# Group statistics of a GroupNorm by a lane shuffle and copies on VectorE in place of products, in a two-layer attention kernel

## The chip, the cores and the metric

One core of one Trainium2 chip runs the whole program. The metric is the device time of one execution in microseconds (us); lower is better. Engines are named as in the profile: PE is TensorE's matmul (PEld its weight load), DVE is VectorE, ACT is ScalarE, POOL is GpSimd, SP is SyncE, which here only issues DMAs. Every engine runs its own list of instructions strictly in order and waits for the others on semaphores.

## The reference

Two self-attention blocks one after the other, on x of shape (4, 64, 32, 32), float32. Each block is

```python
h = group_norm(x, 32 groups)          # 2 channels x 1024 pixels in a group; eps 1e-5, then 1e-6
q, k, v = conv1x1(h)                  # 64 -> 64 channels each, with biases
s = softmax(q^T k / sqrt(64))         # 1024 x 1024 for each image
x = x + conv1x1(s v) + bias
```

So there are eight units of work: four images in each of two layers. An image of the second layer needs the finished image of the first.

## The kernel before

**Layout.** An image lies on 128 partitions: partitions 0 to 63 hold the 64 channels of the first 512 pixels, partitions 64 to 127 the same channels of the other 512. A group of two channels therefore lies on four partitions: c, c^1, and the same two 64 further on. 

**Stages of a unit u.**
1. Statistics: DVE takes each partition's mean and variance (`gn_own`, L440 to L444). PE multiplies the means by a constant matrix that averages over a group (`group_mean_of`, L604 to L606); DVE forms the deviation of each partition from it (`gn_about`, L446 to L454); PE averages again (`group_var_of`, L608 to L610); DVE adds epsilon (`gn_var`, L456 to L459); POOL takes the power -0.5 (`root`, L234 to L236); DVE makes the gain and the shift (`gn_affine`, L461 to L470); ACT applies them and writes h (`apply_norm`, L312).
2. PE projects q and k into ps_scores[0] (`project`, L612) and v times the output weights into ps_misc (`project_v`, L622). ACT copies the high parts, DVE the low parts (L472, L479). SP swaps the halves of the keys by DMA.
3. Row maxima: for each of 8 tiles of 128 queries PE forms rough scores into ps_max (`max_scores`, L628) and DVE takes their maximum (`row_max`, L486). There is one ps_max, so PE's tile m waits until DVE has finished tile m-1 (`next_max`, L756). PE turns the maxima (`turn_max`), ACT stages them (`stage_max`), and SP writes them as rows into q_row with two DMAs, one for each half (`place_rows`, L189).
4. Scores: for each of 8 tiles of keys PE forms the exact scores (`scores`, L644) and ACT the exponentials (`exp`, L345). POOL adds the eight tiles up one by one (`add`, L238, seven additions a unit). PE multiplies by the values into ps_attn (`values`, L668).
5. Closing: when POOL's seventh addition is done PE forms the sums of the softmax (`denominators`, L681), ACT copies them, DVE takes reciprocals in four chunks (`reciprocal`, L501), and POOL multiplies and adds the residual (`finish`, L249), which it does between its third and fourth addition of the next unit.

**Order.** All orders are written out by hand. In iteration w of the main loop PE does the scores and values of unit w, the row maxima of unit w+1, the statistics' products and the projections of unit w+2, and the sums of unit w-1. The statistics' products exist in w = 0 to 5 ("prep"): one pair stands between scores tile 0 and tile 1 (L771), the other after tile 1 (L774). DVE's order in an iteration (L541 to L577) is: row_max 2, gn_about, row_max 3, gn_var and gn_affine, row_max 4, reciprocal, row_max 5, reciprocal, the low parts, two reciprocals, row_max 6 and 7, row_max 0 and 1 of the unit after, gn_own of unit w+3. POOL's order (L289 to L295) is: `root(w + 2)`, additions 1 to 3, finish of unit w-1, additions 4 to 7. Since it is in order, the root of iteration w stands behind the seventh addition of iteration w-1.

**Start.** PE runs `keep_warm` products that nobody reads (20, then 16, L711 and L716), around the first products of the statistics and of the weights (`setup`), before it projects unit 0.

The tail (units 6 and 7 and the closing of unit 7) has no statistics in it.

Of the kernel before, what the change touches and what calls it, by code (L numbers as in the profile page):

```python
# [5 lines left out]
ALU = mybir.AluOpType  # L6
# [24 lines left out]
def attention_pair(nc, x, layer_params, consts, out):  # L31
# [16 lines left out]
    GN = 7  # L48

    with ExitStack() as ctx:  # L50
# [15 lines left out]
        const_sb = sb("const_sb", [P, 2 * P])  # L66
        ident, half_group_mean = const_sb[:, 0:P], const_sb[:, P:2 * P]
# [4 lines left out]
        stats6 = sb("stats6", [P, 6])  # L72
        own = sb("own", [P, 2])
        neg_mean = sb("neg_mean", [P, 1])
        dev = sb("dev", [P, 1])
        var_about = sb("var_about", [P, 1])
# [37 lines left out]
        mean_mm = sem("mean_mm")  # L114
        var_mm = sem("var_mm")
# [51 lines left out]
        def last_row(unit):  # L167
            return 32 * (unit // 2 + 1)
# [4 lines left out]
        def _(sp):  # L173
# [15 lines left out]
            def place_rows(u):  # L189
                sp.wait_ge(max_staged, u + 1)  # L190
                if u < 2:
                    sp.wait_ge(rows_zero, u + 1)
                for n in range(2):
                    row = q_row[u % 2][n * C:n * C + 1, :].bitcast(F32).rearrange("p (t n) -> p t n", t=JS)
                    sp.dma_start(row, max_rows[n * JS:(n + 1) * JS, :].bitcast(F32)).then_inc(row_in[u % 2], 16)
# [104 lines left out]
        def _(act):  # L300
            act.dma_start(const_sb[:, :], consts).then_inc(consts_in, 16)
# [137 lines left out]
        def _(dve):  # L439
            def gn_own(u):  # L440
                base = GN * u
                dve.bn_stats(stats6[:, :], xs[:, slot(u)]).then_inc(gn_step, 1)
                dve.wait_ge(gn_step, base + 1)
                dve.bn_aggr(own[:, :], stats6[:, :]).then_inc(gn_step, 1)  # L444

            def gn_about(u):  # L446
                base = GN * u
                dve.wait_ge(mean_mm, u + 1)
                dve.tensor_scalar(neg_mean[:, :], ps_misc[:, 0:1], -2.0, None, ALU.mult).then_inc(gn_step, 1)
                dve.tensor_scalar(dev[:, :], ps_misc[:, 0:1], -2.0, own[:, 0:1],  # L450
                                  ALU.mult, ALU.add).then_inc(gn_step, 1)
                dve.wait_ge(gn_step, base + 4)
                dve.tensor_scalar(var_about[:, :], dev[:, :], dev[:, :], own[:, 1:2],
                                  ALU.mult, ALU.add).then_inc(gn_step, 1)  # L454

            def gn_var(u):  # L456
                dve.wait_ge(var_mm, u + 1)
                dve.tensor_scalar(var_eps[:, :], ps_misc[:, 1:2], 2.0, EPS[u // B],  # L458
                                  ALU.mult, ALU.add).then_inc(var_ready, 1)  # L459
# [59 lines left out]
            gn_own(0)  # L519
            gn_about(0)  # L520
            gn_var(0)
# [3 lines left out]
            gn_own(1)  # L525
            gn_about(1)
# [4 lines left out]
            gn_var(1)  # L531
# [5 lines left out]
            gn_own(2)  # L537
# [3 lines left out]
            for w in range(UNITS):  # L541
# [5 lines left out]
                if prep:  # L547
                    gn_about(w + 2)
                if nxt:
                    row_max(w + 1, 3)  # L550
                if prep:
                    gn_var(w + 2)
                    gn_affine(w + 2)
# [20 lines left out]
                if w + 3 < UNITS:  # L574
                    if w + 3 >= B:
                        dve.wait_ge(final_done, w + 3 - B + 1)
                    gn_own(w + 3)  # L577
# [21 lines left out]
        def _(pe):  # L599
# [3 lines left out]

            def group_mean_of(u):  # L604
                pe.wait_ge(gn_step, GN * u + 2)
                pe.matmul(ps_misc[:, 0:1], half_group_mean, own[:, 0:1], start=True, stop=True).then_inc(mean_mm, 1)  # L606

            def group_var_of(u):  # L608
                pe.wait_ge(gn_step, GN * u + 5)
                pe.matmul(ps_misc[:, 1:2], half_group_mean, var_about[:, :], start=True, stop=True).then_inc(var_mm, 1)  # L610
# [29 lines left out]
            def turn_max(u):  # L640
                pe.wait_ge(max_ready, u + 1)
                pe.transpose(ps_misc[0:TILES, 0:P], neg_max[u % 2][:, :], ident).then_inc(max_turned, 1)
# [69 lines left out]
            pe.wait_ge(consts_in, 16)  # L712
# [167 lines left out]
```

## Time and profile before

| | |
|---|---|
| median of 3 runs | 206.66 us (206.65, 206.66, 210.21) |
| profiled execution | 207.81 us |
| its span from the first to the last instruction | 206.0 us |
| PE busy | 93% of the span |
| DVE, ACT, POOL busy | 66%, 51%, 76% |
| granted TensorE clock, mean | 0.997 |

The profile is of one execution, a little longer than the median. Times inside it are microseconds from the start of its span; the 1.8 us between its time and its span lie outside what the profile shows.

### The profile page before, as it was taken

How to read it: one execution, taken by the hardware profiler on the slowest of the kernel's cores; microseconds unless marked ns; L12 is line 12 of the kernel's file. 1: busy time of each engine (PE TensorE's matmuls, PEld its weight loads, DVE VectorE, ACT ScalarE, POOL GpSimd, SP SyncE). 2: the span in 40 equal slices, each digit the busy share in tenths (PEclk: the TensorE clock that was granted, in tenths of full speed). 3: DMA queues.
4: the chain of work that ended last, by engine and by line, in shares of the span. 5: the costliest groups of instructions: out<-in, count | busy, mean ns of one | idle time of the engine just before them, and what ended most of it. 6: DMA issues, size and time to landing. Idle time of an engine off the chain costs nothing.

```text
span 206.0 us, 3281 instructions
## 1 busy us (share of the span) xinstructions
PE 192.3 (93%) x1248; PEld 104.0 (50%) x1248; DVE 136.1 (66%) x186; ACT 105.1 (51%) x147; POOL 156.0 (76%) x93
## 2 busy tenths in 40 slices
PE   8989887999999999999999999999999997999950
PEld 8956654645455544554644555554555443444410
DVE  1369957556796749775886679567965485007974
ACT  2458435564655557535854375646555363628310
POOL 1244207799599997998799989997999869998913
PEclk9999999999999999999999999999999999999998
DMA  6224020400021000400040004000211000100011
GB/s 198 108 51 97 8 55 0 102 1 5 2 61 44 1 0 11 93 4 0 0 102 4 0 0 103 3 0 2 63 42 52 5 0 0 52 0 3 0 51 51
DMA packets 4719, 7.06 MB, mean 34 GB/s; under 512 B 800, under 2 KB 1760, under 8 KB 4704
## 3 DMA queue, kind: packets, MB, share of 16 engines
q1 hardware_dynamic: 4272, 6.33, 12.2%
q10 hardware_dynamic: 432, 0.53, 0.9%
q8 instruction: 10, 0.16, 0.3%
q14 instruction: 5, 0.04, 0.1%
HBM read 1.58 MB, written 1.05 MB: 13 GB/s over the span
## 4 chain that ended last, share of the span: by engine, by line
PE 77%; DVE 8%; POOL 8%; issue 3%; ACT 2%; POOLq 0%; DVEq 0%; ACTq 0%
PE ps_attn L677 23%; PE ps_max L637 9%; PE ps_scores L657 6%; POOL prob_sum L247 6%; PE ps_scores L661 5%; PE ps_scores L659 5%; PE ps_scores L665 5%; PE ps_scores L617 4%; PE ps_scores L602 4%; PE ps_misc L625 4%; DVE neg_part L490 3%; PE ps_misc L684 3%; DVE prob_sum L516 2%; ACT probs L350 1%; DVE rden L586 1%
## 5 line engine op out<-in xcount | busy, mean ns | idle before, releaser
L247 POOL TENSOR_TENSOR prob_sum<-prob_sum,probs 128x1024 f32<-128x1024 f32 x44 | 104.5, 2375 | 13.3 <-ACT probs L350 9.0
L490 DVE TENSOR_REDUCE neg_part<-ps_max 128x2 f32<-128x1024 f32 x59 | 71.8, 1218 | 34.7 <-PE ps_max L638 34.7
L350 ACT ACTIVATE probs<-ps_scores 128x1024 f32<-128x1024 f32 x64 | 63.0, 1024 | 48.4 <-PE ps_scores L666 45.1
L677 PE MATMUL ps_attn<-probs,vals 128*64 128x512 f32 x256 | 61.9, 604 | 0.0
L506 DVE RECIPROCAL rden<-den 128x128 f32<-128x128 f32 x28 | 25.1, 926 | 14.9 <-ACT den L356 14.9
L637 PE MATMUL ps_max<-keys,q_hi 64*128 64x512 f32 x59 | 27.7, 470 | 3.6 <-DVE neg_part L490 3.0
L677 PEld LDWEIGHTS ps_attn<-probs,vals 128*64 128x64 f32 x256 | 15.8, 136 | 27.3 <-issue 19.9
L638 PE MATMUL ps_max<-keys,q_hi 64*128 64x512 f32 x59 | 27.7, 469 | 0.0
L657 PE MATMUL ps_scores<-q_hi,keys 64*128 64x512 f32 x64 | 26.3, 411 | 0.0
L658 PE MATMUL ps_scores<-q_hi,keys 64*128 64x512 f32 x64 | 26.3, 411 | 0.0
L665 PE MATMUL ps_scores<-q_row,ones_r 64*128 64x512 f32 x64 | 25.0, 391 | 0.0
L666 PE MATMUL ps_scores<-q_row,ones_r 64*128 64x512 f32 x64 | 25.0, 391 | 0.0
L660 PE MATMUL ps_scores<-q_lo,keys 64*128 64x512 f32 x64 | 25.0, 391 | 0.0
L659 PE MATMUL ps_scores<-q_lo,keys 64*128 64x512 f32 x64 | 25.0, 391 | 0.0
L661 PE MATMUL ps_scores<-q_hi,keys 64*128 64x512 f32 x64 | 25.0, 390 | 0.0
L662 PE MATMUL ps_scores<-q_hi,keys 64*128 64x512 f32 x64 | 24.9, 389 | 0.0
L637 PEld LDWEIGHTS ps_max<-keys,q_hi 64*128 64x128 f32 x59 | 10.8, 183 | 24.4 <-DVE neg_part L490 12.4
L236 POOL TENSOR_TENSOR rstd<-var_eps,minus_half 128x1 f32<-128x1 f32 x8 | 4.4, 552 | 23.7 <-DVE var_eps L458 23.7
L247 POOL TENSOR_TENSOR prob_sum<-probs 128x1024 f32<-128x1024 f32 x8 | 19.1, 2388 | 0.0
L657 PEld LDWEIGHTS ps_scores<-q_hi,keys 64*128 64x128 f32 x64 | 11.8, 185 | 4.6 <-ACT probs L350 2.4
L661 PEld LDWEIGHTS ps_scores<-q_hi,keys 64*128 64x128 f32 x64 | 11.8, 184 | 2.5
L665 PEld LDWEIGHTS ps_scores<-q_row,ones_r 64*128 64x128 f32 x64 | 11.8, 184 | 2.5
(88 smaller groups left out, 308.5 us busy)
## 6 DMA issues: line engine op xcount, KB each, us to landing
keys<-keys SPq DMA_DIRECT2D x32, 128.0 KB, 2.3
xs<-x_dram SPq DMA_DIRECT2D x4, 256.0 KB, 4.3
out_dram<-xs SPq DMA_DIRECT2D x3, 256.0 KB, 2.1
layer<-layers_dram ACTq DMA_DIRECT2D x2, 194.5 KB, 4.7
q_row<-max_rows SPq DMA_DIRECT2D x16, 2.0 KB
out_dram<-xs SPq DMA_DIRECT2D x4, 64.0 KB, 1.6
const_sb<-consts_dram ACTq DMA_DIRECT2D x1, 128.0 KB, 3.6
```

Source lines behind the costliest of these rows:

```text
L247: pool.tensor_tensor(prob_sum[u % 2][:, :], first[:, :], probs[t][:, :], ALU.add).then_inc(added, 1)
L350: act.activation(probs[t][:, :], ps_scores[t % 2][:, :], ACT.Exp, scale=SCALE).then_inc(exp_done, 1)
L490: dve.tensor_reduce(neg_part[u % 2][:, at:at + JS + 1:JS], ps[:, :].rearrange("p (h n) -> p h n", h=2), AX.X, ALU.max, negate=True).then_i ...
L506: dve.reciprocal(rden[:, chunk(c)], den[:, chunk(c)]).then_inc(rden_done, 1)
L637: pe.matmul(ps[:, 0:HALF], q[0:C, mine], k[0:C, cols], start=True, stop=True)
L638: pe.matmul(ps[:, HALF:N], q[C:P, mine], k[C:P, cols], start=True, stop=True).then_inc(max_mm, 1)
L657: pe.matmul(left, k[top, a:a + P], q[top, 0:HALF], start=True, stop=False)
L658: pe.matmul(right, k[low, b:b + P], q[low, 0:HALF], start=True, stop=False)
L659: pe.matmul(left, k[top, a:a + P], ql[top, :], start=False, stop=False)
L661: pe.matmul(left, k[top, a + HALF:a + HALF + P], q[top, 0:HALF], start=False, stop=False)
L665: pe.matmul(left, ones_r[top, :], row[top, :], start=False, stop=True)
L677: mm = pe.matmul(ps_attn[half * C:(half + 1) * C, :], v, probs[t][:, cols], start=(t == 0), stop=(t == TILES - 1))
```

## The change

The products of the statistics go, with their semaphores and the averaging matrix. DVE does it all in one function: it takes the six numbers that `bn_stats` leaves on each partition, swaps neighbouring lanes with one shuffle, copies both sets to the other half of the partitions with two copies, and aggregates the four sets in one `bn_aggr`. Epsilon and the negated mean are taken in the same place. The function stands where `gn_own` stood, so it handles unit w+3 at the end of iteration w. `gn_affine` moves up from behind row_max 3 to behind row_max 2. The DMA of the constants brings the identity alone. The two row DMAs become one. At the start PE has 6 idle products in place of 16. POOL's and ACT's orders are not touched.

```diff
+    PAIRED = [lane ^ 1 for lane in range(32)]
...
-        const_sb = sb("const_sb", [P, 2 * P])
+        ident = sb("ident", [P, P])
...
-            return 32 * (unit // 2 + 1)
+            return 16 * (unit // 2 + 1)
...
-                for n in range(2):
-                    row = q_row[u % 2][n * C:n * C + 1, :].bitcast(F32).rearrange("p (t n) -> p t n", t=JS)
-                    sp.dma_start(row, max_rows[n * JS:(n + 1) * JS, :].bitcast(F32)).then_inc(row_in[u % 2], 16)
+                rows = q_row[u % 2][0:P:C, :].bitcast(F32).rearrange("p (t n) -> p t n", t=JS)
+                sp.dma_start(rows, max_rows[:, :].bitcast(F32)).then_inc(row_in[u % 2], 16)
...
-            act.dma_start(const_sb[:, :], consts).then_inc(consts_in, 16)
+            act.dma_start(ident[:, :], consts[:, 0:P]).then_inc(consts_in, 16)
...
-            def gn_own(u):
+            def gn_group(u):
                 base = GN * u
-                dve.bn_stats(stats6[:, :], xs[:, slot(u)]).then_inc(gn_step, 1)
+                if u:
+                    dve.wait_ge(gn_step, base)
+                    dve.wait_ge(rstd_ready, u)
+                dve.bn_stats(stats[:, 0:STATS], xs[:, slot(u)]).then_inc(gn_step, 1)
                 dve.wait_ge(gn_step, base + 1)
+                dve.stream_shuffle(stats[:, STATS:2 * STATS], stats[:, 0:STATS], PAIRED).then_inc(gn_step, 1)
+                dve.wait_ge(gn_step, base + 2)
+                dve.tensor_copy(stats[0:C, 2 * STATS:4 * STATS], stats[C:P, 0:2 * STATS])
+                dve.tensor_copy(stats[C:P, 2 * STATS:4 * STATS], stats[0:C, 0:2 * STATS]).then_inc(gn_step, 1)
+                dve.wait_ge(gn_step, base + 3)
+                dve.bn_aggr(group[:, :], stats[:, :]).then_inc(gn_step, 1)
                 dve.wait_ge(gn_step, base + 4)
+                dve.tensor_scalar(var_eps[:, :], group[:, 1:2], EPS[u // B], None, ALU.add).then_inc(var_ready, 1)
+                dve.tensor_scalar(neg_mean[:, :], group[:, 0:1], -1.0, None, ALU.mult).then_inc(gn_step, 1)
...
-            def gn_var(u):
-                dve.wait_ge(var_mm, u + 1)
-                dve.tensor_scalar(var_eps[:, :], ps_misc[:, 1:2], 2.0, EPS[u // B],
-                                  ALU.mult, ALU.add).then_inc(var_ready, 1)
...
             dve.wait_ge(x_in[0], 16)
-            gn_own(0)
-            gn_about(0)
-            gn_var(0)
+            gn_group(0)
             dve.wait_ge(params_in[0], 16)
             gn_affine(0)
             dve.wait_ge(x_in[1], 16)
-            gn_own(1)
-            gn_about(1)
+            gn_group(1)
...
-            gn_var(1)
...
             dve.wait_ge(x_in[2], 16)
-            gn_own(2)
+            gn_group(2)
...
                 if nxt:
                     row_max(w + 1, 2)
                 if prep:
-                    gn_about(w + 2)
+                    gn_affine(w + 2)
                 if nxt:
                     row_max(w + 1, 3)
-                if prep:
-                    gn_var(w + 2)
-                    gn_affine(w + 2)
                 if nxt:
                     row_max(w + 1, 4)
...
-                    gn_own(w + 3)
+                    gn_group(w + 3)
...
             keep_warm(20)
-            pe.wait_ge(consts_in, 16)
-            group_mean_of(0)
             setup(0)
-            group_var_of(0)
-            keep_warm(16)
-            group_mean_of(1)
+            keep_warm(6)
             project(0)
-            group_var_of(1)
             max_scores(0, 0, ps_max)
             max_scores(0, 1, ps_scores[1])
             pe.wait_ge(setup_done, 1)
-            pe.wait_ge(var_ready, 2)
             project_v(0)
...
             setup(1)
+            pe.wait_ge(consts_in, 16)
             pe.wait_ge(v_copied, 2)
             turn_max(0)
...
-                if prep:
-                    pe.wait_ge(max_staged, w + 1)
-                    group_mean_of(w + 2)
                 scores(w, 1)
-                if prep:
-                    group_var_of(w + 2)
                 next_max(3)
                 if w:
                     values(w - 1, 6)
                     values(w - 1, 7)
                     if prep:
-                        pe.wait_ge(var_ready, w + 3)
+                        pe.wait_ge(max_staged, w + 1)
                         denominators(w - 1)
...
                     project(w + 2)
                     if w:
                         pe.wait_ge(den_copied, w)
+                    else:
+                        pe.wait_ge(max_staged, 1)
                     project_v(w + 2)
```

## Rows read from the trace of the kernel before

**Rows 1.** The page's part 2: PE's busy tenths in 40 slices of 5.15 us.

```profile
PE   8989887999999999999999999999999997999950
```

**Rows 2.** Chain that ended last, from 49 to 76: start, length, piece of it.

```profile
55.51 0.23 PE ps_scores L657
...
71.15 0.31 PE ps_misc L606 x2
71.46 0.43 PE ps_scores L657
...
72.58 0.31 PE ps_misc L610 x2
72.90 0.42 PE ps_max L637
```

**Rows 3.** Timeline of POOL: start, duration, line, tiles, [idle before <-releaser].

```profile
41.43 9.96 POOL L247 TENSOR_TENSOR prob_sum<-prob_sum,probs 128x1024 f32<-128x1024 f32 x4 [1.54 <-ACT probs L350]
...
64.38 9.94 POOL L247 TENSOR_TENSOR prob_sum<-prob_sum,probs 128x1024 f32<-128x1024 f32 x4
74.73 0.55 POOL L236 TENSOR_TENSOR rstd<-var_eps,minus_half 128x1 f32<-128x1 f32 x1 [0.42 <-DVE var_eps L458]
...
83.67 1.29 POOL L253 TENSOR_TENSOR attn<-attn,rden 128x512 f32<-128x512 f32 x1 [0.24 <-DVE rden L506]
```

**Rows 4.** Timeline of DVE from 54 to 84, same columns.

```profile
54.62 1.23 DVE L490 TENSOR_REDUCE neg_part<-ps_max 128x2 f32<-128x1024 f32 x1 [0.67 <-PE ps_max L638]
...
69.11 0.69 DVE L442 BATCH_NORM_STATS2 stats<-xs 128x6 f32<-128x512 f32 x1
...
70.26 1.23 DVE L490 TENSOR_REDUCE neg_part<-ps_max 128x2 f32<-128x1024 f32 x1 [0.25 <-PE ps_max L638]
...
75.32 0.21 DVE L467 TENSOR_SCALAR gain<-rstd,layer 128x1 f32<-128x1 f32 x1 [0.66 <-POOL rstd L236]
75.57 0.27 DVE L469 TENSOR_SCALAR shift<-neg_mean,gain,layer 128x1 f32<-128x1 f32 x1
76.52 1.23 DVE L490 TENSOR_REDUCE neg_part<-ps_max 128x2 f32<-128x1024 f32 x1 [0.68 <-PE ps_max L638]
...
81.84 1.75 DVE L506 RECIPROCAL rden<-den 128x128 f32<-128x128 f32 x2
```

**Rows 5.** Timeline of iteration w = 0, DVE, ACT and PE.

```profile
27.96 1.23 DVE L490 TENSOR_REDUCE neg_part<-ps_max 128x2 f32<-128x1024 f32 x1 [1.40 <-PE ps_max L638]
...
32.99 1.22 DVE L490 TENSOR_REDUCE neg_part<-ps_max 128x2 f32<-128x1024 f32 x1
33.10 0.82 ACT L316 ACTIVATE h<-xs,shift,gain 128x512 f32<-128x512 f32 x1 [2.75 <-DVE shift L469]
...
34.79 1.23 DVE L490 TENSOR_REDUCE neg_part<-ps_max 128x2 f32<-128x1024 f32 x1 [0.59 <-PE ps_max L638]
34.88 0.64 PE L617 MATMUL ps_scores<-h,layer 64*64 64x512 f32 x1
```

**Rows 6.** Timeline of the start, several engines.

```profile
4.10 0.69 DVE L442 BATCH_NORM_STATS2 stats<-xs 128x6 f32<-128x512 f32 x1 [4.10 <-DMA xs<-x_dram]
...
7.37 3.44 PE L602 MATMUL ps_scores<-ones 128*64 128x64 f32 x32
...
7.79 0.55 POOL L236 TENSOR_TENSOR rstd<-var_eps,minus_half 128x1 f32<-128x1 f32 x1 [6.45 <-DVE var_eps L458]
...
9.01 0.81 ACT L316 ACTIVATE h<-xs,shift,gain 128x512 f32<-128x512 f32 x1 [1.33 <-DVE shift L469]
...
11.05 0.64 PE L617 MATMUL ps_scores<-h,layer 64*64 64x512 f32 x1
```

**Rows 7.** Line L602 (idle products): duration min/median/max in ns.

```profile
L602 PEld LDWEIGHTS ps_scores<-ones x72: 138/227/232, 0.9 to 10.5; 128*64 128x64 f32 x72
```

**Rows 8.** Groups by line and shape, of DVE's additions at the end.

```profile
L516 DVE TENSOR_TENSOR prob_sum<-prob_sum,probs 128x1024 f32<-128x1024 f32 x2 | 4.1, 2038 | 0.3 <-ACT probs L350 0.2
...
L516 DVE TENSOR_TENSOR prob_sum<-probs 128x1024 f32<-128x1024 f32 x1 | 2.7, 2746 | 0.8 <-ACT probs L350 0.8
```

More of the change, by code:

```diff
@@ L48, in attention_pair @@
     GN = 7
+    STATS = 6
+    PAIRED = [lane ^ 1 for lane in range(32)]
     with ExitStack() as ctx:
@@ L65, in attention_pair @@
         bias_k = [sb(f"bias_k{n}", [P, 1]) for n in range(LAYERS)]
-        const_sb = sb("const_sb", [P, 2 * P])
-        ident, half_group_mean = const_sb[:, 0:P], const_sb[:, P:2 * P]
+        ident = sb("ident", [P, P])
         ones = sb("ones", [P, C])
@@ L70, in attention_pair @@
         minus_half = sb("minus_half", [P, 1])
-        stats6 = sb("stats6", [P, 6])
-        own = sb("own", [P, 2])
+        stats = sb("stats", [P, 4 * STATS])
+        group = sb("group", [P, 2])
         neg_mean = sb("neg_mean", [P, 1])
-        dev = sb("dev", [P, 1])
-        var_about = sb("var_about", [P, 1])
         var_eps = sb("var_eps", [P, 1])
@@ L113, in attention_pair @@
         gn_step = sem("gn_step")
-        mean_mm = sem("mean_mm")
-        var_mm = sem("var_mm")
         var_ready = sem("var_ready")
@@ L439, in _ @@
         def _(dve):
-            def gn_own(u):
+            def gn_group(u):
                 base = GN * u
-                dve.bn_stats(stats6[:, :], xs[:, slot(u)]).then_inc(gn_step, 1)
+                if u:
+                    dve.wait_ge(gn_step, base)
+                    dve.wait_ge(rstd_ready, u)
+                dve.bn_stats(stats[:, 0:STATS], xs[:, slot(u)]).then_inc(gn_step, 1)
                 dve.wait_ge(gn_step, base + 1)
[L444 to L451, printed above, removed]
-                dve.wait_ge(gn_step, base + 4)
-                dve.tensor_scalar(var_about[:, :], dev[:, :], dev[:, :], own[:, 1:2],
-                                  ALU.mult, ALU.add).then_inc(gn_step, 1)
-            def gn_var(u):
-                dve.wait_ge(var_mm, u + 1)
-                dve.tensor_scalar(var_eps[:, :], ps_misc[:, 1:2], 2.0, EPS[u // B],
-                                  ALU.mult, ALU.add).then_inc(var_ready, 1)
+                dve.stream_shuffle(stats[:, STATS:2 * STATS], stats[:, 0:STATS], PAIRED).then_inc(gn_step, 1)
[4 more added lines that the diff above has]
+                dve.bn_aggr(group[:, :], stats[:, :]).then_inc(gn_step, 1)
+                dve.wait_ge(gn_step, base + 4)
+                dve.tensor_scalar(var_eps[:, :], group[:, 1:2], EPS[u // B], None, ALU.add).then_inc(var_ready, 1)
+                dve.tensor_scalar(neg_mean[:, :], group[:, 0:1], -1.0, None, ALU.mult).then_inc(gn_step, 1)
             def gn_affine(u):
@@ L602, in keep_warm @@
                     pe.matmul(ps[0:C, 0:C], ones[:, :], ones[:, :], start=True, stop=True)
[L604 to L610, printed above, removed]
             def project(u):
@@ L641, in turn_max @@
                 pe.wait_ge(max_ready, u + 1)
-                pe.transpose(ps_misc[0:TILES, 0:P], neg_max[u % 2][:, :], ident).then_inc(max_turned, 1)
+                pe.transpose(ps_misc[0:TILES, 0:P], neg_max[u % 2][:, :], ident[:, :]).then_inc(max_turned, 1)
             def scores(u, t):
```

## The prediction, made before the changed kernel was run

> **What bounds the kernel now.** I read the page's slices first, then the chain of waits, then the timelines of the other engines against PE's. In the slices PE is at nine tenths or more from the eighth slice to the thirty-third; only the start and the last units are looser [rows 1]. In the chain of a middle unit every piece is PE's, so the unit lasts as long as PE's list of instructions. The same row maximum comes every 76.52 - 54.62 = 21.90 us [rows 4]. The products of the statistics are in that chain. A pair takes 0.31, and the product behind it takes 0.43 or 0.42 in place of the 0.23 of one that follows its own kind [rows 2].
>
> The second engine is POOL. Its seventh addition of a unit ends at 64.38 + 9.94 = 74.32, and it then stands idle for only 0.42, until DVE's variance releases the root at 74.73 [rows 3]. I call the end of the seventh addition E. The reader is to see where the result of that root is wanted: DVE's gain starts at 75.32, 0.59 behind the root's start, after row maximum 3 is done and ahead of row maximum 4 [rows 4]. So the wait costs nothing now.
>
> **The change, iterations 1 to 5.** PE loses two pairs: 0.31 + (0.43 - 0.23) + 0.31 + (0.42 - 0.23) = 1.01 a unit [rows 2]. Were PE still the bound, the unit would last 20.89.
>
> It will not be. Statistics are now made a unit ahead, so the root no longer waits for DVE; but it still stands behind POOL's seventh addition, and gn_affine, which wants it, now stands ahead of row maximum 3. DVE waits there with row maxima 3 and 4 queued behind it, then the reciprocals and the low parts. PE's tile 4 waits for row maximum 3, and PE's scores 2 and 3 stand behind tile 4. From E on:
> - root at E (0.4 earlier than now), gain 0.59 later, shift 0.25 after the gain (75.57 - 75.32) [rows 4], row maximum 3 about 0.2 later (an estimate: the shift's 0.27, partly overlapped): E + 1.04.
> - row maximum 4 comes 1.80 after row maximum 3 when PE waits for DVE between them (34.79 - 32.99) [rows 5]: E + 2.84. Now it starts at 76.52, E + 2.20 [rows 3, 4].
> - from row maximum 4, DVE is busy through the reciprocals until 81.84 + 1.75 = 83.59 [rows 4]; POOL's finish waits for them and starts at 83.67 [rows 3]; the next E follows four additions later. One unit earlier the same path is 54.62 to 74.32, so 19.70.
> The loop then closes through POOL: 2.84 + 19.70 = 22.54 a unit against 21.90, 0.64 slower. Left alone, PE would bring row maximum 4 at 76.52 + 20.89 = 97.41; by way of POOL it comes at 76.52 + 19.70 + 2.84 = 99.06. So the way by POOL decides, and PE has 1.65 to spare.
>
> The first of these units is different: its E is 41.43 + 9.96 = 51.39 [rows 3], early against PE. Row maximum 4 comes at 51.39 + 2.84 = 54.23 in place of 54.62 [rows 4], 0.39 earlier. Four more units at 0.64 make +2.56. Sum for w = 1 to 5: +2.17. Units 6 and 7 have no statistics and move as a whole.
>
> **DVE's new function.** Shuffle, copies, aggregate and two scalings are not in the trace. The nearest rows are the small operations beside them, which come every 0.25 (gain to shift); the far ends are 0.1 and the 0.69 of the statistics instruction itself [rows 4]. With 0.25 for shuffle and aggregate, 0.3 for the two copies and 0.25 for the scalings the function takes 1.75 in place of 0.9, since row maximum 2 starts 1.15 behind the statistics with 0.25 idle [rows 4]. It then starts 0.6 later. That is within PE's 1.65 of new slack, so it costs nothing here, nor would twice as much; if PE were the bound it would cost some 0.2 a unit.
>
> A rule speaks against the copies. DVE's first addition at the end takes 2746 ns beside a busy POOL, and the two others 2038 ns [rows 8], so the two engines may disturb each other, by a third. The Trainium skill, "Advanced Engine Details and Errata", section "VectorE Performance Modes", says more: VectorE's second SBUF port is shared with GpSimd, and instructions that use it block each other. Float copies inside SBUF would be such. By the row the copies cost 0.1 more; what a real block would do is a rival below.
>
> **Iteration 0.** POOL is idle here, so the root is early and the wait costs nothing. Tile 3 no longer waits for a product that waited for DVE: row maximum 3 can follow row maximum 2 by 1.80, at 29.76. Row maximum 4 follows at 31.56; now it starts at 32.99, behind gain and shift [rows 5]. Exponential 2 is now held back by h, which ends at 33.92. The projection starts 34.88 - 33.92 = 0.96 behind that. Afterwards both hang on the scores: tile 4 on PE at 29.76 + 1.28 = 31.04, its 0.42, four score pieces of 0.23 [rows 2], so the exponential starts at 32.4; PE's own list, with four more pieces and tile 5, reaches the projection at 33.5. I take 33.6 in place of 34.88 [rows 5]: 1.3 earlier. If the scores or ACT take longer than counted, it is down to 0.8, what tile 3 alone gives.
>
> **Start.** Statistics start at 4.10. Then 0.73, shuffle 0.25, copies 0.3, aggregate 0.25: epsilon at 5.63, root at about 5.9 in place of 7.79, h 1.22 behind it (9.01 - 7.79), so 7.15 to 7.97. PE's projection now starts at 11.05, because PE is in idle products until 7.37 + 3.44 = 10.81, though h was done at 9.82 [rows 6]. With 6 in place of 16 they end by about 7.7, and the projection starts at 8.05: 3.0 earlier, 1.8 of it from h, 1.2 from idle products. All behind it moves along. If the new instructions cost 0.1 or 0.69 each, this is 3.4 or 1.6.
>
> **Row DMA and constants.** The rows are staged some 5 us before the scores want them, so one DMA in place of two changes no end; at nothing on either side. The smaller constants free at most some 0.1 us of DMA at the start.
>
> **Sum.** 207.81 - 3.0 - 1.3 + 2.17 = 205.7 us. The profiled execution is 1.15 above the median. I take this for the idle products: their weight loads took 227 ns in the middle and 138 ns at the end [rows 7], which are TensorE's levels of 1.2 and 2.4 GHz, while the granted clock reads full throughout. At the upper level the 3.44 us would be 2.1, the projection would start when h ends, and 1.2 would be saved. The changed kernel no longer waits on them, so against the median only 1.0 us is left, 0.5%.
>
> **Rivals.**
> - *PE stays the bound* (the affine's wait is covered by something I overlook). Full gain: 5 x 1.01 = 5.05, giving 207.81 - 3.0 - 1.3 - 5.05 = 198.5; with POOL's addition chain holding PE a little, 200.5. For it: PE's solid chain. Against it: the root starts at E, and nothing in the diff moves it.
> - *Slower than before: a slow TensorE at the start.* With ten idle products fewer the first real products run at 1.2 GHz. It decides when the level has not risen by 8.05. The first projection then lasts 1.0 longer: 206.7. In slices 3 to 5 PE is about 85% busy [rows 1]; if the level stays low until 17 us, half of 9 x 0.85 is lost, 3.8: 209.5. For it: 72 loads were mostly slow until 10 us [rows 7]. Against it: shorter executions of the same kernel exist.
> - *The copies are blocked* for as long as an addition of POOL, 9.94 / 4 = 2.5 [rows 3]. Row maximum 2 is late by 0.6 + 2.5 and passes PE's slack of 1.65 by 1.4 a unit, in five units 7: 212.5. This is what the rule named above would make of it; the trace shows a third, not a block [rows 8].
>
> **How the numbers follow.** Forecast as summed 0.52; slow first projection only 0.15; slow until 17 us 0.13; PE or POOL bound with the gain kept 0.11; blocked copies or other costs above 210.8 0.05; the rest spread within 2%. The forecast's own range is 204.3 to 206.8 (loop cost 0.64 plus or minus 0.2 in five units, start 1.6 to 3.4). With most of the slow starts the range is 203.6 to 208.6. A measurement tells about 2% from no change: faster by over 2% 0.11, within 0.84, slower 0.05.
>
> **What would show it.** Right: no PE work between scores 0 and 1; DVE idle 2 to 3 us before the gain, released by POOL's root, ahead of row maximum 3; PE idle over 1 us before tile 4 of the row maxima; units of 22.5 us; POOL nearly without idle time; the first projection near 8 us, loads of 138 ns there. Wrong: units of 21.3 or less, or the gain not waiting.

## The result: slower, not unchanged

| | before | after |
|---|---|---|
| median, us (executions) | 208.44 (4) | 213.37 (4) |
| from, to | 206.65 to 210.47 | 211.75 to 214.66 |
| profiled execution / its span | 207.81 / 206.0 | 212.3 / 210.5 |
| mean granted TensorE clock of it | 0.997 | 0.967 |

After over before is 1.0296, with a 95% interval of 1.0176 to 1.0417: clearly slower, though the interval reaches below 2%. This ratio is of fast executions alone, so it is not the quotient of the two medians, which the executions of the kernel before at 210.21 and 210.47 move. The forecast was 205.7 us, range 203.6 to 208.6. The four executions of the kernel before are the three shown earlier and one more, 210.47, which takes its median from 206.66 to 208.44, halfway between two pairs. The profiled executions, from which the working starts, differ by 4.5 us where a gain of 2.1 was forecast: 6.6 us are to be found. Of the changed kernel's other executions one took 211.75, and two took 214.4 and 214.7 at a granted clock of 0.952; of these there is no profile.

The page of the kernel after: from its part 2 (a slice is 5.26 us, and the PE row answers to [rows 1]), and the lines of the chain that ended last, part 4:

```profile
PE   8699879989998899969999699969999997999950
...
PEclk9999999999999799997999999996999999999996
...
PE ps_attn L654 21%; PE ps_max L614 8%; DVE neg_part L482 7%; POOL prob_sum L243 6%; PE ps_scores L634 4%; DVE stats L445 4%; PE ps_scores L594 4%; PE ps_scores L636 4%; PE ps_misc L602 4%; PE ps_scores L642 4%; PE ps_scores L638 4%; PE ps_misc L661 4%; DVE stats L441 2%; DVE prob_sum L508 2%; DMA xs<-x_dram 2%
```

PE, which was solid in the middle of [rows 1], now has a dent in each unit (8 and 8 where it falls on two slices, then three times 6). And the granted clock falls to 7, 7 and 6 tenths in three slices, each behind or in such a dent. The chain has a line of DVE that was not expected in it, L445, with 4% of the span or 8 us.

L445 is the first of the two copies of `gn_group`. The timeline of DVE after, with the columns of [rows 4], to which it answers (line 482 is `row_max`, 459 the gain, 461 the shift):

```profile
64.70 0.68 DVE L441 BATCH_NORM_STATS2 stats<-xs 128x6 f32<-128x512 f32 x1
...
65.42 0.16 DVE L443 STREAM_SHUFFLE stats<-stats 128x6 f32<-128x6 f32 x1
65.61 1.85 DVE L445 COPY stats<-stats 64x12 f32<-64x12 f32 x1
67.48 0.17 DVE L446 COPY stats<-stats 64x12 f32<-64x12 f32 x1
67.68 0.26 DVE L448 BATCH_NORM_AGGREGATE group<-stats 128x2 f32<-128x24 f32 x1
...
68.11 1.22 DVE L482 TENSOR_REDUCE neg_part<-ps_max 128x2 f32<-128x1024 f32 x1
70.47 0.21 DVE L459 TENSOR_SCALAR gain<-rstd,layer 128x1 f32<-128x1 f32 x1 [1.14 <-POOL rstd L232]
70.72 0.27 DVE L461 TENSOR_SCALAR shift<-neg_mean,gain,layer 128x1 f32<-128x1 f32 x1
70.91 1.22 DVE L482 TENSOR_REDUCE neg_part<-ps_max 128x2 f32<-128x1024 f32 x1
74.78 1.23 DVE L482 TENSOR_REDUCE neg_part<-ps_max 128x2 f32<-128x1024 f32 x1 [2.65 <-PE ps_max L615]
```

Two copies of one size stand side by side, and the first takes 1.85 us, the second 0.17. POOL at the same time, in the columns of [rows 3]:

```profile
59.98 9.95 POOL L243 TENSOR_TENSOR prob_sum<-prob_sum,probs 128x1024 f32<-128x1024 f32 x4
69.88 0.55 POOL L232 TENSOR_TENSOR rstd<-var_eps,minus_half 128x1 f32<-128x1 f32 x1
```

The four additions follow each other every 9.95 / 4 = 2.5 us from 59.98, so the third ends near 67.45. The copy ends at 67.46. The row for line 445 over the whole trace says that this is a pattern:

```profile
L445 DVE COPY stats<-stats x8: 168/1270/1854, 5.0 to 137.6; 64x12 f32<-64x12 f32 x8
```

The first copies of the start, where POOL does nothing, take 0.17 us; those from 65.61 on take 1.81 to 1.85. One takes 0.73, and it is the one that tells most, beside POOL's additions of that time:

```profile
43.88 0.73 DVE L445 COPY stats<-stats 64x12 f32<-64x12 f32 x1
...
37.17 9.93 POOL L243 TENSOR_TENSOR prob_sum<-prob_sum,probs 128x1024 f32<-128x1024 f32 x4 [1.64 <-ACT probs L346]
```

Four additions take 9.93, so the third ends near 37.17 + 3 x 2.48 = 44.61. The copy began later in its addition, waited less, and ends at 44.61: the length differs, the place of the end does not. The second copy is never long. So the first is held until POOL's running addition is over, and its neighbour goes through with it. `gn_group` takes 3.4 us, and row maximum 2 starts at 68.11, 1.7 later than without the hold. PE waits for it, and what PE does next is the second finding. Its timeline behind that wait, and two units later:

```profile
69.38 0.50 PE L614 MATMUL ps_max<-keys,q_hi 64*128 64x512 f32 x1 [1.73 <-DVE neg_part L482]
...
69.82 3.02 PE L654 MATMUL ps_attn<-probs,vals 128*64 128x512 f32 x8
72.62 1.69 PE L661 MATMUL ps_misc<-prob_sum,ones 128*64 128x512 f32 x4
...
118.47 0.49 PE L614 MATMUL ps_max<-keys,q_hi 64*128 64x512 f32 x1 [1.70 <-DVE neg_part L482]
...
118.89 1.94 PE L654 MATMUL ps_attn<-probs,vals 128*64 128x512 f32 x8
120.66 1.03 PE L661 MATMUL ps_misc<-prob_sum,ones 128*64 128x512 f32 x4
```

Eight value products take 3.02 us and four for the denominators 1.69; at 118 us, behind an idle time of 1.70, the same groups take 1.94 and 1.03. The table of windows gives the granted clock for each microsecond (the number behind POOL's busy time; 1.00 is 2.4 GHz and 0.50 is 1.2 GHz):

```profile
68.00:69.00 1.00, 0.00 (x0) 0.00 (x0) 1.00 (x3) 0.72 (x1) 1.00 (x1) 1.00 0.00 0
...
70.00:71.00 1.00, 1.00 (x6) 0.24 (x6) 0.49 (x3) 0.00 (x0) 1.00 (x2) 0.76 0.00 0
71.00:72.00 1.00, 1.00 (x6) 0.39 (x4) 1.00 (x1) 0.00 (x0) 1.00 (x1) 0.50 0.06 16
72.00:73.00 1.00, 1.00 (x4) 0.26 (x3) 0.12 (x1) 0.12 (x1) 0.74 (x1) 0.50 0.00 0
```

PE did nothing from 68 to 69, worked again from 69.38, and from about 70.5 its clock is at 1.2 GHz for over 3 us. The same follows at 94 and at 142 us. Row maximum 4 starts at 50.23, 74.78, 99.34, 122.16 and 146.70: units of 24.55, 24.56, 22.82 and 24.54, where 22.54 was forecast. A fall thus costs 24.55 - 22.82 = 1.73, three of them 5.2. The held copy alone costs 22.82 - 22.54 = 0.28, four times 1.1. Together these are 6.3 of the 6.6 us. The other 0.3 lies ahead of the first of these row maxima: by the forecast's terms it was due at 54.62 - 3.0 - 1.3 - 0.39 = 49.93, and it starts at 50.23.

### The profile page after: what moved, and what is told of

The parts are those of the page before. It is cut to its first block, busy times and chain, and to the rows that moved or that the text cites. A ratio compares the mean times of both kernels' runs of the same rounds, so it can differ in the third digit from the quotient of the medians.

```text
span 210.5 us, 3184 instructions
## 1 busy us (share of the span) xinstructions
PE 188.0 (89%) x1196; PEld 97.6 (46%) x1196; DVE 143.8 (68%) x202; ACT 104.6 (50%) x147; POOL 155.7 (74%) x93
## 4 chain that ended last, share of the span: by engine, by line
PE 63%; DVE 19%; POOL 8%; issue 5%; ACT 2%; DMA 2%; POOLq 0%; DVEq 0%; ACTq 0%
PE ps_attn L654 21%; PE ps_max L614 8%; DVE neg_part L482 7%; POOL prob_sum L243 6%; PE ps_scores L634 4%; DVE stats L445 4%; PE ps_scores L594 4%; PE ps_scores L636 4%; PE ps_misc L602 4%; PE ps_scores L642 4%; PE ps_scores L638 4%; PE ps_misc L661 4%; DVE stats L441 2%; DVE prob_sum L508 2%; DMA xs<-x_dram 2%
## 5 line engine op out<-in xcount | busy, mean ns | idle before, releaser
L654 PE MATMUL ps_attn<-probs,vals 128*64 128x512 f32 x256 | 66.0, 639 | 0.0
L498 DVE RECIPROCAL rden<-den 128x128 f32<-128x128 f32 x28 | 25.1, 927 | 14.9 <-ACT den L352 14.9
L654 PEld LDWEIGHTS ps_attn<-probs,vals 128*64 128x64 f32 x256 | 16.4, 140 | 28.5 <-issue 22.5
L634 PE MATMUL ps_scores<-q_hi,keys 64*128 64x512 f32 x64 | 25.6, 399 | 0.0
L635 PE MATMUL ps_scores<-q_hi,keys 64*128 64x512 f32 x64 | 25.6, 399 | 0.0
L638 PE MATMUL ps_scores<-q_hi,keys 64*128 64x512 f32 x64 | 24.9, 390 | 0.0
L639 PE MATMUL ps_scores<-q_hi,keys 64*128 64x512 f32 x64 | 24.9, 389 | 0.0
L360 ACT ACTIVATE attn<-ps_attn 128x512 f32<-128x512 f32 x8 | 4.8, 598 | 26.3 <-PE ps_attn L654 26.3
L634 PEld LDWEIGHTS ps_scores<-q_hi,keys 64*128 64x128 f32 x64 | 11.9, 185 | 4.4 <-ACT probs L346 2.4
```

Of the source, the lines that this page charges most:

```text
L498: dve.reciprocal(rden[:, chunk(c)], den[:, chunk(c)]).then_inc(rden_done, 1)
L634: pe.matmul(left, k[top, a:a + P], q[top, 0:HALF], start=True, stop=False)
L635: pe.matmul(right, k[low, b:b + P], q[low, 0:HALF], start=True, stop=False)
L638: pe.matmul(left, k[top, a + HALF:a + HALF + P], q[top, 0:HALF], start=False, stop=False)
L654: mm = pe.matmul(ps_attn[half * C:(half + 1) * C, :], v, probs[t][:, cols], start=(t == 0), stop=(t == TILES - 1))
```

## Experiments

Ratios are to the kernel before, run in turn with the experiment on the same chip, and a range in brackets behind a ratio is its 95% interval. A unit is measured between two reciprocals or two fourth row maxima that stand a unit apart in the profile.

### 1. The affine back behind row maximum 3

```
-                if prep:
-                    gn_affine(w + 2)
                 if nxt:
                     row_max(w + 1, 3)
+                if prep:
+                    gn_affine(w + 2)
```

> The changed kernel with gn_affine put back behind row maximum 3. Theory A (the first copy is held by GpSimd's running addition for up to 1.85 us, row maximum 2 comes late, and TensorE's idle time behind it lowers the clock): nothing that binds is touched, units stay at 22.8 or 24.5 us, time 211.5 to 214.5. Theory B (the gain's wait for the root is what costs): row maximum 4 no longer waits for E + 2.8, five units gain 0.6 or more each, time at most 209.5.

Measured: 214.25 us (213.25 to 214.59), 1.0229 of the kernel before (1.0146 to 1.0312). No gain over the 213.37 of the kernel after. The copies are held as before, and row maximum 3 now starts 0.60 behind row maximum 2 with no gain between them, yet row maximum 4 comes no sooner: 77.12 is 7.45 behind the start of the held copy, and in the unit of the kernel after that had no fall of the clock it is 122.16 - 114.74 = 7.42.

```profile
69.67 1.83 DVE L445 COPY stats<-stats 64x12 f32<-64x12 f32 x1
...
72.15 1.22 DVE L482 TENSOR_REDUCE neg_part<-ps_max 128x2 f32<-128x1024 f32 x1
73.96 1.23 DVE L482 TENSOR_REDUCE neg_part<-ps_max 128x2 f32<-128x1024 f32 x1 [0.60 <-PE ps_max L615]
75.10 0.20 DVE L459 TENSOR_SCALAR gain<-rstd,layer 128x1 f32<-128x1 f32 x1
...
77.12 1.23 DVE L482 TENSOR_REDUCE neg_part<-ps_max 128x2 f32<-128x1024 f32 x1 [1.50 <-PE ps_max L615]
```

The wait on which the forecast hung is covered by the held copy and by the products that PE has behind it, at full clock too. Whether it is there at all needs the copies out of the way.

### 2. Shuffles in place of the copies

```
-                dve.tensor_copy(stats[0:C, 2 * STATS:4 * STATS], stats[C:P, 0:2 * STATS])
-                dve.tensor_copy(stats[C:P, 2 * STATS:4 * STATS], stats[0:C, 0:2 * STATS]).then_inc(gn_step, 1)
+                for quarter in range(4):
+                    to, frm = quarter * 32, (quarter * 32 + C) % P
+                    mm = dve.stream_shuffle(stats[to:to + 32, 2 * STATS:4 * STATS],
+                                            stats[frm:frm + 32, 0:2 * STATS], SAME)
+                mm.then_inc(gn_step, 1)
```

`SAME` is `list(range(32))`: the shuffle moves the same bytes and permutes nothing.

> The changed kernel with the two copies across the halves made by four 32-lane shuffles with an identity mask. Theory A: a shuffle is not held by GpSimd, so none of them takes over 0.3 us, row maximum 2 is no longer late, TensorE waits 1.3 us at tile 4 instead (for the root and the affine), units take 22.5 us as forecast, and if the clock holds the time is 205.6; with the clock down in some units up to 209. Theory B: no gain beyond 1 us, 211 or more. If shuffles are held as copies are: the same times as the changed kernel.

Measured: 208.78 us (207.57 to 210.21, 10 executions), 1.005 of before (1.0005 to 1.0095): 4.6 us below the kernel after. DVE's timeline (line 448 is the new shuffle, the first of the four shown; the last row is POOL's root):

```profile
67.40 0.16 DVE L448 STREAM_SHUFFLE stats<-stats 32x12 f32<-32x12 f32 x1
...
68.57 1.22 DVE L486 TENSOR_REDUCE neg_part<-ps_max 128x2 f32<-128x1024 f32 x1
72.23 0.21 DVE L463 TENSOR_SCALAR gain<-rstd,layer 128x1 f32<-128x1 f32 x1 [2.44 <-POOL rstd L233]
...
72.67 1.22 DVE L486 TENSOR_REDUCE neg_part<-ps_max 128x2 f32<-128x1024 f32 x1
74.48 1.23 DVE L486 TENSOR_REDUCE neg_part<-ps_max 128x2 f32<-128x1024 f32 x1 [0.59 <-PE ps_max L619]
...
71.64 0.55 POOL L233 TENSOR_TENSOR rstd<-var_eps,minus_half 128x1 f32<-128x1 f32 x1
```

The shuffles are not held, though POOL runs its additions from 61.74 to 71.64. The forecast's picture appears line by line: the gain waits 2.44 us for POOL's root with row maximum 3 queued behind it, row maximum 3 starts 72.67 - 71.64 = 1.03 after the root, which stands directly behind the seventh addition (forecast 1.04), row maximum 4 2.84 after it (forecast 2.84). The units are 22.49, 22.48, 22.48 and 22.51 against 22.54. PE's idle time comes in two pieces, 0.43 and 0.87, and no unit has a fall of the clock. There is one in iteration 0, from 29.8 to 33.2 us, which experiment 6 takes up:

```profile
30.00:35.00 5.00, 5.00 (x28) 2.57 (x28) 1.97 (x3) 3.26 (x5) 3.75 (x2) 0.68 0.01 3
```

The profiled execution is the shortest of the ten, 207.57. Four of the others took 210.0 or more at a granted clock of 0.97; where they lost it no profile shows.

### 3. Both

The edits of experiments 1 and 2 together.

> Four shuffles in place of the copies and gn_affine behind row maximum 3. Theory A with the forecast's own second step (the gain's wait is the next bound once the copies are free): both waits gone, units at 21.3 us, held by GpSimd's additions, or 20.9, held by TensorE, time 199 to 201.5. If the wait for the root had no price, this equals the kernel with the shuffles alone.

Measured: 204.61 us (203.98 to 205.89), 0.9792 of before (0.9719 to 0.9865), units of 21.54 to 21.57. Moving the affine, worth nothing with held copies, is worth 4.2 us without them: the two waits lay over each other, and only the longer one was to be seen. The time stays above the 199 to 201.5 that was expected, and the units above 21.3. What is left ahead of row maximum 2 is `gn_group` itself, 66.93 to 69.05 in this profile, 2.1 us against the 0.9 of before, and PE is idle for 0.44 us behind it; iteration 0 has the same slow stretch as in experiment 2.

### 4. The clock alone: idle products in PE's wait

The kernel after, held copies and all, with work for PE while it waits:

```
                 scores(w, 1)
+                if w and prep:
+                    pe.wait_ge(max_staged, w + 1)
+                    keep_warm(12, ps_misc)
                 next_max(3)
```

> The changed kernel with 12 idle products into a free bank behind scores tile 1 in iterations 1 to 5, where TensorE stands idle for 1.7 us. Theory A, second half (idle time lowers the clock): granted clock at 0.99 or more, no values at half speed, all units at 22.8 us, time 207.1. If the lower clock has another cause: it still falls, time 211.5 to 214.5.

Measured: 208.77 us (207.81 to 211.81, 10 executions), 1.0048 of before (1.0002 to 1.0095), 4.6 below the kernel after. PE's timeline, to be read beside that of the kernel after (line 587 is the idle products, its records counted double):

```profile
70.64 1.61 PE L587 MATMUL ps_misc<-ones 128*64 128x64 f32 x24
72.41 0.49 PE L614 MATMUL ps_max<-keys,q_hi 64*128 64x512 f32 x1 [0.15 <-DVE neg_part L482]
...
72.83 1.94 PE L654 MATMUL ps_attn<-probs,vals 128*64 128x512 f32 x8
```

The first copy still takes 1.82 us (68.67 to 70.49). But the value products take 1.94 in every unit, and the units are 22.80 to 22.85, the length of the one unit of the kernel after that had no fall. Products whose result nobody reads brought 4.6 us, by which the second loss is shown to be the clock, and the idle time of PE to have a part in it. Its size is confirmed between the fourth row maxima of the first and the last of these units: 96.47 us in the kernel after, 144.61 - 53.30 = 91.31 here, 5.2 less.

The time is above the 207.1 that was expected, for two reasons that the profile shows. Iteration 1 has an idle time of only 0.60, and the idle products stretch it: from the held copy of iteration 0 to the first of those row maxima it is 53.30 - 46.09 = 7.21, against 50.23 - 43.88 = 6.35, 0.9 more. And this profiled execution, 210.21, has its clock at 1.2 GHz from 8.1 to 14.9 us, which the kernel after had not:

```profile
10.00:15.00 5.00, 4.50 (x21) 3.19 (x22) 3.31 (x4) 3.32 (x7) 2.49 (x2) 0.51 0.25 55
```

The first copy of iteration 0 comes at 25.82 in place of 23.61, 2.2 later. Without that the execution would be at 208.0; the two shortest were 207.81 and 207.96, at a granted clock of 0.994.

### 5. Which instructions are held

Three kernels change only how the two halves are exchanged.

`e_odd`, the copies written as 4 rows of 3 and read as 3 rows of 4:

```
+                for to, frm in ((slice(0, C), slice(C, P)), (slice(C, P), slice(0, C))):
+                    mm = dve.tensor_copy(stats[to, 2 * STATS:4 * STATS].rearrange("p (a b) -> p a b", a=4),
+                                         stats[frm, 0:2 * STATS].rearrange("p (a b) -> p a b", a=3))
```

> The changed kernel with the same two copies, but each written as 4 rows of 3 elements and read as 3 rows of 4, so the two halves of the pattern can't be split alike. If the copy is held because it takes a second port in two halves, as the Trainium skill says under VectorE Performance Modes, it is no longer held: 0.2 us each, and the kernel behaves like the one with shuffles, units 22.5 us, 206 to 210. If any copy inside SBUF is held while GpSimd works, or the crossing of the halves is what is held: 1.8 us as before, 211.5 to 214.5.

Measured: 212.43 us (210.11 to 213.49), 1.0174 of before (1.0073 to 1.0276). The pair of copies takes 1.97 to 2.02 us in iterations 1 to 4, 0.35 at the start: the hold is there. It settles nothing: both patterns are contiguous and may well reach the engine as plain rows of 12.

`e_pitch`, written to a tile of its own at a pitch of 5, so that the pattern can't be joined:

```
+                    mm = dve.tensor_copy(spread[to, :].rearrange("p (a b) -> p a b", b=5)[:, :, 0:4],
+                                         stats[frm, 0:2 * STATS].rearrange("p (a b) -> p a b", b=4))
...
-                dve.bn_aggr(group[:, :], stats[:, :]).then_inc(gn_step, 1)
+                dve.bn_aggr(group[:, :], stats[:, 0:2 * STATS]).then_inc(gn_step, 1)
```

It leaves the other half of the pixels out of the group's statistics; the instructions are the same but for an aggregate of 12 values in place of 24 (0.21 us against 0.26).

> The changed kernel, where the two copies write 3 rows of 4 elements at a pitch of 5 into a tile of their own, and the aggregate reads the two sets of its own half only (the statistics leave out the other half of the pixels). The pattern written has 3 rows, an odd number, and can't be merged with the one read. If the rule of the Trainium skill names the cause (the instruction runs in two halves over both ports), the copies are not held: 0.2 us each, units 22.5 us. If a copy is held whatever its pattern: the first takes up to 1.85 us in iterations 1 to 4.

Measured: 205.25 us, one execution, before 206.02. All copies of the trace, and those two beside POOL's additions of 59.34 to 69.27:

```profile
L447 DVE COPY spread<-stats x16: 159/160/161, 4.6 to 132.6; 64x12 f32<-64x12 f32 x16
```

```profile
64.98 0.33 DVE L447 COPY spread<-stats 64x12 f32<-64x12 f32 x2
65.35 0.21 DVE L451 BATCH_NORM_AGGREGATE group<-stats 128x2 f32<-128x12 f32 x1
...
69.82 0.21 DVE L462 TENSOR_SCALAR gain<-rstd,layer 128x1 f32<-128x1 f32 x1 [2.87 <-POOL rstd L233]
```

A copy of the same 12 values between the same partitions is not held when it is written in this way. The pattern and the tile that is written changed together; which of the two counts is not shown. The units are 22.49 to 22.50, and the clock is 0.993.

`e_tt`, a maximum of each value with itself in place of the copy:

```
+                    mm = dve.tensor_tensor(stats[to, 2 * STATS:4 * STATS], stats[frm, 0:2 * STATS],
+                                           stats[frm, 0:2 * STATS], ALU.max)
```

> The changed kernel with each copy written as a tensor_tensor maximum of a set with itself, which reads two sources. If what is held is the use of the second port at all, this is held as the copy is, 1.8 us. If it is the splitting of one source over two ports, or the copy's own instruction, it is not held: 0.2 to 0.3 us, units of 22.5 us.

Measured: 208.85 us, one execution. The pair, beside POOL's additions:

```profile
65.61 2.00 DVE L446 TENSOR_TENSOR stats<-stats 64x12 f32<-64x12 f32 x2
```

It is held as the copy is (at the start, without POOL, the pair takes 0.35), and the units are 22.83, 22.85, 22.84 and, with a fall of the clock, 24.53: the two lengths of the kernel after. So the hold belongs neither to copies alone nor to exchanges between partitions as such, which the shuffles and `e_pitch` make unheld. The Trainium skill, "VectorE: DVE Perf Modes", section "Why `tensor_tensor` can't do 2×_2P or 4×", has an operation on two tensors read its second operand through port 1, which by the page named next would be the shared one; the row agrees. That page of the Trainium skill, "Advanced Engine Details and Errata", section "VectorE Performance Modes", has VectorE use a second read port where source and destination lie in SBUF and the outermost dimension longer than one is even in both, or odd and equal, and says that such instructions and GpSimd's block each other. `e_pitch` fits that if its source is joined to one row of 12 while its destination keeps 3 rows. What these runs show is that the form of the copy decides; that it does so through a port is the page's account.

### 6. Further down: the statistics moved, the row DMA, iteration 0

`e_moved` is experiment 3 with `gn_group(w + 2)` issued behind row maximum 2 for w of 1 and more, in place of `gn_group(w + 3)` at the end of the iteration before:

```
                 if nxt:
                     row_max(w + 1, 2)
+                if w and prep:
+                    if w + 2 >= B:
+                        dve.wait_ge(final_done, w + 2 - B + 1)
+                    gn_group(w + 2)
...
-                if w + 3 < UNITS:
-                    if w + 3 >= B:
-                        dve.wait_ge(final_done, w + 3 - B + 1)
-                    gn_group(w + 3)
```

> Shuffles, gn_affine behind row maximum 3, and gn_group of unit w+2 behind row maximum 2 of iteration w in place of unit w+3 at the end of the iteration before. Theory: what still held units at 21.57 us was the length of gn_group ahead of row maximum 2; behind it, it falls into DVE's idle time. Units at 20.9 to 21.3 us, TensorE without idle time there, five units gain 0.3 to 0.6 each: 1.5 to 3 below the kernel with both edits, 202 to 203. If GpSimd's additions hold at 21.5 anyway: the same time.

Measured: 204.92 us (200.95 to 205.38), before 207.43; with three executions at 204.9 to 205.4 and one at 200.95 no ratio is given. Units of 21.42 and 21.43, only 0.13 below those of experiment 3, where 20.9 to 21.3 was expected. Part 4 of its page says why:

```profile
POOL prob_sum L244 34%; PE ps_attn L658 9%; DVE neg_part L486 5%; PE ps_max L618 5%; PE ps_misc L665 4%; POOL attn L250 3%; POOL xs L253 3%; PE ps_scores L638 3%; ACT probs L347 3%; PE ps_scores L640 3%; PE ps_scores L642 3%; PE ps_scores L646 3%; PE ps_scores L598 3%; PE ps_misc L606 2%; DVE prob_sum L512 2%
```

POOL's additions now hold the chain. The four executions spread over 4.4 us, and the lowest has the highest clock, 0.996 against 0.966 to 0.973; the profiled one falls at the start (8.3 to 15.1 us) and in iteration 0 (32.2 to 35.6).

`e_best` is `e_moved` with 13 idle products at the start in place of 6, and two groups of them in iteration 0:

```
                 scores(w, 1)
+                if w == 0:
+                    pe.wait_ge(max_staged, 1)
+                    keep_warm(6, ps_misc)
                 next_max(3)
+                if w == 0:
+                    keep_warm(9, ps_misc)
...
-            keep_warm(6)
+            keep_warm(13)
```

> The kernel before this one in the list, with 13 idle products in place of 6 at the start and 6 and 9 more in iteration 0, where TensorE stands idle for 0.9 and 1.3 us. Theory (idle time of over a microsecond lets the clock fall in a part of the executions, each fall costs 1 to 2 us): granted clock at 0.99 or more in all executions, spread under 1 us, median 1 to 2 below the kernel without them, 200 to 201.5. If the falls have nothing to do with idle time: clock 0.98 to 0.99 as before, same median.

Measured: 202.13 us (201.2 to 202.9), 0.9715 of before (0.9645 to 0.9784): faster than both kernels. Expected were 200 to 201.5, a spread under 1 us and a clock of 0.99 or more; the clocks are 0.944, 0.986, 0.991 and 0.986. Three of the four executions of `e_moved` are above all four of this kernel, its fourth, 200.95, is below them all. So the idle products are likely to help, but with four executions each it is not shown that they remove the falls.

`e_tworows` is experiment 3 with the two row DMAs of the kernel before:

```
-                rows = q_row[u % 2][0:P:C, :].bitcast(F32).rearrange("p (t n) -> p t n", t=JS)
-                sp.dma_start(rows, max_rows[:, :].bitcast(F32)).then_inc(row_in[u % 2], 16)
+                for n in range(2):
+                    row = q_row[u % 2][n * C:n * C + 1, :].bitcast(F32).rearrange("p (t n) -> p t n", t=JS)
+                    sp.dma_start(row, max_rows[n * JS:(n + 1) * JS, :].bitcast(F32)).then_inc(row_in[u % 2], 16)
```

> Shuffles and gn_affine behind row maximum 3, with the row DMA written as two again. The rows are wanted some 5 us after they are staged, so no step waits for the second DMA: units at 21.57 us as with one. If the single DMA had brought something, units are longer by up to its 0.65 us of issue.

Measured: 205.29 us in one execution, units of 21.56 to 21.57 as with one DMA. The DMA edit is worth nothing in the units; this execution has a fall at 10.6 to 14.0 us, too, that the profile of experiment 3 has not.

## Why the prediction was wrong, and where it was right

**Wrong: "By the row the copies cost 0.1 more".** This is the step that failed. It priced the copies beside a busy POOL from DVE's long additions at the end [rows 8], and took the third between the first and the other two as proof against the rule which stood next to it. Measured is a hold to the end of the running addition, 1.6 to 1.7 us on top of 0.17.

The row was misread. All three additions ran beside a busy POOL, and laid against POOL's own rows of the kernel before they show the hold already:

```profile
171.52 1.28 POOL L253 TENSOR_TENSOR attn<-attn,rden 128x512 f32<-128x512 f32 x1
...
186.93 4.91 POOL L247 TENSOR_TENSOR prob_sum<-prob_sum,probs 128x1024 f32<-128x1024 f32 x2 [0.54 <-ACT probs L350]
191.79 2.26 POOL L253 TENSOR_TENSOR attn<-attn,rden 128x512 f32<-128x512 f32 x1
194.13 2.13 POOL L256 TENSOR_TENSOR xs<-attn,xs 128x512 f32<-128x512 f32 x1
...
190.17 2.75 DVE L516 TENSOR_TENSOR prob_sum<-probs 128x1024 f32<-128x1024 f32 x1 [0.82 <-ACT probs L350]
193.17 4.18 DVE L516 TENSOR_TENSOR prob_sum<-prob_sum,probs 128x1024 f32<-128x1024 f32 x2 [0.25 <-ACT probs L350]
```

POOL's instructions end at 191.84, 194.05 and 196.26. DVE's additions end at 192.92, 195.15 and 197.35 (the first of the pair takes 1.97): each time 1.1 after POOL's. Each looks like an addition of about 1.1 us (an estimate from these distances; none ran beside an idle POOL) that waited first, 1.7, 0.9 and 1.0. And POOL's two instructions, which take 1.28 elsewhere, take 2.26 and 2.13, so POOL is held by DVE as well. The two sizes, 2746 and 2038 ns, differ by how far POOL's instruction had come. By the Trainium skill's rule the rival "The copies are blocked" was written down, with 212.5 us and a share of 0.05; its mechanism is what happened, and it deserved a good deal more.

**Wrong: no price for an idle TensorE in mid-kernel.** The working treated 1.65 us of slack on PE as free, "nor would twice as much" cost anything. Filled up, this slack became one idle stretch of 1.7 us, behind which the granted clock fell in three of four units, 1.73 us each. Experiment 4 shows it. With the same hold and the same idle time it fell in two of four units in experiment 1, and in one of four each in `e_odd` and `e_tt`, so it is a cost that comes and goes. The slow TensorE was thought of for the start alone. In experiment 2 the same unit has its idle time in pieces of 0.43 and 0.87, and the clock holds.

**The rival's 212.5 came near 212.3 by luck.** It had the hold cost 1.4 a unit (205.7 and 7 would even be 212.7); alone it cost 0.28, since what is left of the hold runs beside the wait for POOL's root. The rest is the clock, which it did not have.

**Right: the wait of the affine.** "19.70 to next E: unit 22.54" became 22.50 in experiment 2 and 22.49 in `e_pitch`, where nothing is held. `e_pitch` with a clock of 0.993 took 205.25 us in its one execution, 0.8 below the kernel before beside it: about the forecast's 205.7, and about its gain of 1.0, with the whole change in place but for the other half of the pixels in the statistics. In the kernel after, this wait is hidden below the other two, so that undoing it alone changes nothing.

**Right: start and iteration 0.** The first projection is at 8.07 (forecast 8.05), where [rows 6] had 11.05:

```profile
8.07 0.64 PE L594 MATMUL ps_scores<-h,layer 64*64 64x512 f32 x1 [1.11 <-ACT h L312]
```

That of iteration 0 is at 30.63, 4.25 before that of [rows 5] and 30.6 by the sum (33.6 - 3.0).

**Partly right: the rival of a slow TensorE at the start.** It did not come in this profile, but it did in those of experiments 1 and 4 and of `e_moved`, which have the same 6 idle products: the clock is at 1.2 GHz from about 8 to about 15 us. It was priced at 3.8 us for a level low until 17 us; measured in experiment 4 are 2.2. The changed kernel's own executions at 214.4 and 214.7 have the granted clock of the profiled execution of experiment 1, 0.952, and are 2.1 and 2.4 above 212.3. That they lost it in the same way is likely and not shown.

**Right: small terms.** Shuffle 0.16, unheld copies 0.17, aggregate 0.26: with the unit's other instructions 1.7 for `gn_group` where it isn't held, 1.75 forecast. The row DMA is worth nothing.

**Not settled.** In experiments 2 and 3 the clock fell in iteration 0, behind idle times of PE of 0.87 and 1.32. In the profiles of the kernel after, `e_tt` and `e_pitch`, with 0.47 and 1.32, it did not, but in those of experiment 1 and `e_odd`, which have these two as well, it did; what decides is not known. Nor was it tried why the kernels of experiment 6 end at 21.43 a unit rather than below 21.3, beyond the chain's word that POOL holds them.

## What to carry to other kernels

Before a small elementwise instruction is put on VectorE beside a busy GpSimd, ask whether it could be held until GpSimd's running instruction ends; price it at up to the length of that instruction, and prefer a form that isn't held, as here a shuffle. To read from a trace whether two engines hold each other, lay the ends of one engine's instructions against the other's; a mean duration hides it. Slack on TensorE is not free to the last tenth: if it comes in one piece, the clock may fall, in some executions and not in others, and a few idle products in the gap are a cheap test of that. And where two waits overlap, undoing one shows nothing; an experiment that frees the other first shows both.

## What the runs showed of the hardware that was not expected

- A held VectorE instruction gets in between two of GpSimd's additions, and the next of its kind goes through unheld: 1.85 then 0.17 us, with GpSimd's four additions at 9.95 us as before (9.94). Statistics, aggregates, one-column scalings and shuffles, beside the same additions, take the time that they take at the start.
- VectorE and GpSimd hold each other in both directions: at the end of the kernel before, GpSimd's multiplication of 1.28 us takes 2.26 beside VectorE's long additions.
- TensorE's clock fell to 1.2 GHz behind idle stretches of 1.73, 1.72 and 1.65 us in units that were otherwise busy, and not behind one of 1.70 among them. In `e_tt` it did not fall behind 1.69, 1.72 and 1.69, and fell behind 1.71. So the length of the stretch alone does not decide.
- The profiled execution of `e_best` has a granted clock of 0.95, between the two levels, in every stretch from 6 us to the end of PE's work, on one core, and is still within 0.3% of its median. No run here explains it:

```profile
30.00:35.00 5.00, 5.00 (x36) 2.28 (x32) 2.99 (x4) 3.71 (x5) 3.69 (x2) 0.95 0.04 10
...
100.00:105.00 5.00, 5.00 (x35) 2.65 (x33) 3.24 (x5) 2.84 (x4) 4.70 (x3) 0.95 0.26 57
```
